# Layer-1 attention blocks with and without six TensorE products whose results nobody reads

## The reference, cut to what matters

```
q = x@Wq + bq;  k = x@Wk + bk;  v = x@Wv + bv
Q = elu(q) + 1;  K = elu(k) + 1
KV = sum over rows of K*v;  Ksum = sum over rows of K
Z = 1 / (Q*Ksum + 1e-6);  V = Q * KV * Z
attn = gelu(V@Wo + bo)
x = layernorm(attn + x) * ln1_s + ln1_b
h = gelu(x@Wf1 + bf1)
ff = gelu(h@Wf2 + bf2)
x = layernorm(ff + x) * ln2_s + ln2_b
```

## Time and profile before

| | |
|---|---|
| median of three runs | 1970.92 us |
| the profiled execution, its own time | 1969.74 us |
| its span in the trace | 1968.0 us |
| what lies around the span | 1.7 us |
| TensorE (PE) busy | 1720.7 us, 87% |
| VectorE (DVE) busy | 1353.3 us, 69% |
| ScalarE (ACT) busy | 1137.2 us, 58% |
| GpSimd (POOL) busy | 285.7 us, 15% |
| layer-1 blocks, first L1819 to eighth L1819 | 1192.48 to 1625.60 us |
| products of L1819 | 48, as 96 records |

### The profile page before, as it was taken

One profiled execution on the slowest core, in us unless ns is written; L12 is line 12 of the kernel. 1 busy time (PEld: TensorE's weight loads), 2 busy tenths in 40 slices (PEclk: granted clock), 3 DMA queues, 4 the chain that ended last, 5 costly groups with the idle time before them and its releaser, 6 DMA issues.

```text
span 1968.0 us, 28168 instructions
## 1 busy us (share of the span) xinstructions
PE 1720.7 (87%) x10420; PEld 770.0 (39%) x10420; DVE 1353.3 (69%) x2656; ACT 1137.2 (58%) x2091; POOL 285.7 (15%) x364
## 2 busy tenths in 40 slices
PE   5898139699999999999979988999989998799999
PEld 4788137122222222222234434444444444444443
DVE  6998876899999999999724356565665656522222
ACT  5465003279989999998863345665566655222222
POOL 4456001400000000000000011111111111111111
PEclk8999658589999999999989989999999999799999
DMA  1000000122100000000012320000000000312441
GB/s 51 1 1 1 0 0 2 39 38 35 17 2 2 2 2 2 2 2 2 18 28 52 91 41 1 17 17 2 15 17 17 17 0 1 43 34 49 48 56 31
DMA packets 72528, 39.12 MB, mean 20 GB/s; under 512 B 22113, under 2 KB 68705, under 8 KB 72401
## 3 DMA queue, kind: packets, MB, share of 16 engines
q1 hardware_dynamic: 71824, 36.65, 10.4%
q10 hardware_dynamic: 576, 0.79, 0.1%
HBM read 34.08 MB, written 3.15 MB: 19 GB/s over the span
## 4 chain that ended last, share of the span: by engine, by line
PE 60%; DVE 28%; ACT 4%; issue 3%; DMA 2%; POOL 1%; SPq 1%; DVEq 0%; ACTq 0%; POOLq 0%
DVE MX L1144 17%; PE PS L1711 6%; PE PS L1226 6%; PE PS L1717 6%; PE PS L2226 4%; PE PS L2227 4%; PE PS L2236 4%; PE PS L1662 4%; PE PS L1252 4%; PE PS L539 3%; PE PS L1681 2%; PE PS L1103 2%; PE PS L1819 2%; DMA SB<-scr_w 2%; DVE MS L643 2%
## 5 line engine op out<-in xcount | busy, mean ns | idle before, releaser
L1285 ACT ACTIVATE tmpb<-PS 128x512 f32<-128x512 f32 x1024 | 554.1, 595 | 76.1 <-PE PS L1252 56.9
L1144 DVE TENSOR_REDUCE MX<-PS 128x2 f32<-128x1024 f32 x512 | 584.5, 1216 | 17.8 <-PE PS L1103 15.9
L1226 PE MATMUL PS<-tmpb,VS 128*32 128x256 f32 x4096 | 327.8, 392 | 1.5 <-ACT tmpb L1285 0.6
L1103 PE MATMUL PS<-KST,QST 56*128 56x512 bf16 x1024 | 205.4, 399 | 18.5 <-DVE MX L1144 16.7
L1252 PE MATMUL PS<-QST,KST 59*128 59x512 bf16 x1024 | 200.6, 388 | 3.8 <-ACT tmpb L1285 1.0
L2261 DVE TENSOR_TENSOR HG<-HG,PS 128x512 f32<-128x512 f32 (+1 forms) x96 | 65.9, 686 | 183.1 <-PE PS L2227 183.1
L2251 ACT ACTIVATE HG<-PS 128x512 f32<-128x512 f32 (+1 forms) x96 | 57.2, 595 | 186.6 <-PE PS L2226 186.6
L1226 PEld LDWEIGHTS PS<-tmpb,VS 128*32 128x32 f32 x4096 | 80.8, 108 | 195.9 <-issue 108.4
L1252 PEld LDWEIGHTS PS<-QST,KST 59*128 59x128 bf16 x1024 | 49.5, 93 | 222.5 <-ACT tmpb L1285 209.0
L1711 PE MATMUL PS<-X,WF 128*128 128x512 f32 x256 | 124.3, 620 | 3.8 <-ACT X L1907 3.7
L1923 ACT ACTIVATE HF<-PS,CL 128x512 f32<-128x512 f32 x128 | 87.9, 687 | 64.6 <-PE PS L1711 64.6
(11 more groups left out here) (335 smaller groups left out, 2528.6 us busy)
## 6 DMA issues: line engine op xcount, KB each, us to landing
SB<-scr_w SPq DMA_DIRECT2D x14, 1024.0 KB, 14.6
WF<-in_L_attn_Wf SPq DMA_DIRECT2D x16, 256.0 KB, 3.1
QST<-NMP SPq DMA_DIRECT2D x192, 1.0 KB
G<-in_L_ffn_w SPq DMA_DIRECT2D x16, 176.0 KB, 2.4
W<-in_L_ffn_w SPq DMA_DIRECT2D x16, 128.0 KB, 2.2
QST<-scr_q SPq DMA_DIRECT2D x14, 128.0 KB
scr_q<-tmpb SPq DMA_DIRECT2D x3, 512.0 KB, 3.6
KST<-scr_k SPq DMA_DIRECT2D x14, 96.0 KB
```

What stands on the lines that cost most here:

```text
L1103: pe.matmul(PS[:, b + x, :], QST[r, 2 * g + jj, CH * qc + P * t:CH * qc + P * t + P], KST[r, g, cs(kc)], start=True, stop=True).then_inc(s ...
L1144: r = v.tensor_reduce(MX[:, :, m // (TPC * NC), m // NC % TPC, m % NC], PS[:, b:b + 2, :], AX.X, ALU.max)
L1226: last = pe.matmul(PS[32 * j:32 * j + 32, 3, h], VS[:, kt, u // NC, :], PB[:, kt % 2, j, h], start=(kt == 0 and half == 0), stop=(kt == NT ...
L1285: a.activation(PB[:, kt % 2, j, :], PS[:, at % 3, :], ACT.Exp, scale=HD ** -0.5).then_inc(s_exp, 1)
```

## The change

The constant WARM goes from 6 to 0. The loop at the end of `pe_inputs` then issues nothing, in each of the eight blocks. Nothing else differs; no wait, buffer or semaphore is touched.

```
--- before.py
+++ after.py
@@ -1627,7 +1627,7 @@
         s_bxt, s_x3 = sem("s_bxt"), sem("s_x3")
         COLS = ("bq", "bk", "bv", "ln1_s", "ln1_b", "ln2_s", "ln2_b", "bo", "bf2")
         BQ, BK, BV, C1, B1, C2, B2, BO, BF2, BF1 = range(10)
-        WARM = 6
+        WARM = 0
         LW = (4 + 2 + len(COLS) + KF) * 16
         EPS_Z = 1e-6
```

## The result

Six runs of the changed kernel took 1981.62 to 1987.13 us, median 1984.3; the kernel before, run beside them, 1968.33 to 1976.2, median 1972.25. The ratio is 1.0061, with a 95% interval of 1.0042 to 1.008: slower by 0.6%. The profiled execution took 1983.41 us, its span is 1981.7. The forecast was 1985.5, 15.8 us over the profiled execution before; the two profiled executions lie 13.67 us apart, the medians 12.05.

What follows compares the result with a forecast made beforehand. At the six products the ScalarE and VectorE chain was taken as the bound, then a chain of latencies. Removed work 0, low clock 13.1 and later low stretches 2.7 added 15.8 us to 1969.74: 1985.5, range 1972 to 1995.

Steps and rivals of the forecast that it cites:

- The six products hide beside ScalarE and VectorE and are worth nothing in themselves: Start of each layer-1 block: removing 42.5 us of TensorE work gains 0, at most 0.8 us in all.
- The wait of 4.7 us brings the clock down in every block: Before WO2's products: the new empty wait drops the clock to 0.50, back some 4 to 7 us later.
- what was read from the long waits: Two earlier waits of 5.3 to 6.0 us: clock stayed low 6.9 and 6.5 us after TensorE resumed.
- the case set down as a rival for all blocks: Short low stretch at WO2: a block loses 0.6 to 1.03 us, time 1977; chance 0.15.
- 1.64 us a block for it: Low clock behind the wait before WO2: 1.03 + 0.15 + 0.46 a block, 13.1 us for eight.
- The 0.15 for the loads: One-column product and weight loads before WO2's first product, slower and no longer hidden: +0.15 us a block, bounds 0 and 0.47.
- 1.03: First product of WO2 and chunk 0, fully exposed: two passes take 2.05 us at 1.2 GHz against 1.02.
- 0.46, as predicted: Y's four transposes, if the clock is still low: 1.06 us against 0.60, +0.46 a block.
- What is late next: 2.7 us: Wait before each block's second transposes: low stretch follows in four of eight blocks instead of two, +2.7 us.
- 1.33: Price in us of one low stretch behind the wait before a block's second transposes.
- 15.8 forecast: Whole kernel: 13.1 + 2.7 us over the profiled execution's 1969.74 us, giving 1985.5; chance 0.50 for 1979 to 1988.
- The rule of the Trainium skill: Y's transposes would take as long at either clock, making the low-clock cost 9.4 us; the trace disagreed, 1.06 against 0.60.

Runs made afterwards that it cites:

- eight products: Eight unread products instead of six behind the last input product, against the kernel before: 1992.46 us, ratio 1.0107.
- the second trace: The changed kernel profiled once more with no edit: 1986.7 us.
- three products, first block: First block of the run with three unread products instead of six, issued at once, against the kernel before: 1980.63 us, ratio 1.0051.
- three well-placed ones: Three unread products instead of six, held back until VectorE's last Q is finished, against the kernel before: 1972.4 us, ratio 1.0006.

## Why the prediction was right

- *The six products hide beside ScalarE and VectorE and are worth nothing in themselves*: right. L1677's start against L2000 moved by 0.02 us, and one product more than six costs its 0.85 us (eight products).
- *The wait of 4.7 us brings the clock down in every block*: right, 4.71 us, and 16 of 16 blocks in two traces. The long low stretches lasted up to 5.8 us past L2000's start (6.4 in the second trace), near what was read from the long waits. In blocks 2, 5 and 8 the clock was still at 1.00 when TensorE took up work again and fell 0.7 to 1.0 us after L2000's start; the stretch was short, the case set down as a rival for all blocks.
- *1.64 us a block for it*: too large. The 0.15 for the loads is nothing (L1677 waits for the tanh meanwhile; three products, first block, show it at the full clock). The first product cost 0.95 where the whole stage was low, not 1.03, and Y's transposes 0.46, as predicted: 1.41 in place of 1.64. Where the low stretch was short, 0.87 to 0.95. The sum of the table's third column is 9.6 us, not 13.1.
- *What is late next: 2.7 us*: too small for this pair of traces. Five of eight blocks instead of four, and each cost 1.5 to 1.7 us (its length less 61.49 less the third column: 63.99 gives 1.63), not 1.33, since they fell into the dense feed-forward products. Five at 1.6 (the last block's, which can't be measured, taken like the others) make 8.0, less 2.65 is +5.4.
- *The sum*: 9.6 + 5.4 = 15.0 for 15.8 forecast. Two errors of about 3 us with opposite signs made it look better than it was; that is luck. Beside them the span has -2.35 us from before the first block, and +1.2 from the stage behind the last one, whose low stretch was 23.9 us instead of 20.5 in two pieces: about 13.8 us for 13.7 measured. The -2.35 belongs to the executions: the first L2000 starts at 1197.02 and 1193.81 us in the two traces before, at 1194.67 and 1197.39 in the two after.
- *The sum, by medians*: the second pair of traces lies 21.7 us apart (1965.03 and 1986.7), so that no single pair can confirm 15.8. With the second wait open, the medians differ by 12.05 us (1972.25 and 1984.3); with it filled, by 10.0 (1965.66 and 1975.67), which is the price at WO2 and near the table's 9.6. About 2 us are left for what is late next, where this pair of traces has 5.4; the interval of the first difference, 8.3 to 15.8 us, can't tell the two apart. Filling the second wait alone took 6.8 us from the kernel before (1972.5 to 1965.66), worth about five stretches at the prediction's 1.33 (an estimate from these medians; their interval allows two to six), so that the two of the trace before may be fewer than is usual.
- *The rule of the Trainium skill ("TensorE: Matmul & The Clock Gate", section on PE-mode transpose) that the full clock doesn't engage for transposes*: the trace after disagrees as that of before did: 1.12 us for Y's four at 0.50, 0.60 at 1.00.

## What to carry to other kernels

Before taking out work that nobody reads, look at what its engine does in that time without it and at the granted clock behind waits of such length: here 42 us of useless products were free, and the empty place cost 12 us. Such filler has to end where the next real work begins, no later (0.85 us a product), and products of one partition did not serve as filler (1998.69 us). When one wait has been filled, look for the next where the clock falls: three products in the second wait of each block gave 0.3% over the kernel that had been tuned, and three well-placed ones did what six did in the first.

## What the hardware showed that was not expected

- The clock fell while TensorE was 100% busy, with products of one partition (1.00 to 1259.5 and 0.50 from there, no idle between).
- A wait of 2.14 us before the thin start of a block let it fall in eight of eight blocks, one of 1.83 us with dense products behind it in none, and the wait of 2.75 us before the second transposes in one or two of eight with six products, five with five, and eight with eight. The length of a wait alone does not tell.
- Where the low stretch falls differs from block to block in one execution, and so does its price, 0.87 to 1.41 us for the same wait: a single block must not be taken for all.
